# Splitting the FFN's tokens in place and turning them by DMA transposes, in a fused attention and FFN block

## What is computed

```python
x = x + attn(layernorm(x), W_qk, W_v, slope)      # scores = (x @ W_qk) @ x.T / sqrt(128)
x = x + ffn(layernorm(x), w_gate, w_up, w_down)   #   + (kpos - qpos) * slope, causal, softmax; v = x @ W_v.T
# ffn: h = silu(x @ wg.T) * (x @ wu.T); h @ wd.T   with wg, wu [384, 128], wd [128, 384] from int8-range integers / 127
```

## Time and profile before

| | us |
|---|---|
| median of 3 runs | 145.16 (144.49 to 145.37) |
| the profiled execution, its own time | 145.67 |
| its span, first to last instruction | 143.9 |
| PE busy | 122.8 (85% of the span) |
| DVE busy | 120.7 (84%) |
| ACT busy | 110.7 (77%) |
| POOL busy | 97.6 (68%) |

### The profile page before, as it was taken

The page is one execution under the profiler, slowest core; times in us unless marked ns, Lnnn a source line. Parts: engine busy times, 40 slices in busy tenths (PEclk is TensorE's granted clock), DMA queues, the critical chain, the costliest instruction groups (busy, mean ns, idle before and its releaser), DMA issues.

```text
span 143.9 us, 3450 instructions
## 1 busy us (share of the span) xinstructions
PE 122.8 (85%) x1215; PEld 91.9 (64%) x1215; DVE 120.7 (84%) x341; ACT 110.7 (77%) x251; POOL 97.6 (68%) x157
## 2 busy tenths in 40 slices
PE   0239658999999999999999998979998899999942
PEld 0028345867987769978779776657755656675541
DVE  0729989998697996969996969999879999988781
ACT  4034588999976999949999769985699978999830
POOL 6490769964993454992438943798999999646810
PEclk9999999999999999999999999999999999999995
DMA  4997000000000000000000000000000222022204
GB/s 129 221 244 190 0 0 2 7 2 0 5 0 0 5 0 2 5 0 0 0 5 0 5 0 2 2 5 0 5 0 0 77 77 66 12 73 77 77 0 146
DMA packets 9811, 5.18 MB, mean 36 GB/s; under 512 B 448, under 2 KB 9792, under 8 KB 9792
## 3 DMA queue, kind: packets, MB, share of 16 engines
q1 hardware_dynamic: 9792, 4.92, 12.2%
HBM read 2.82 MB, written 2.10 MB: 34 GB/s over the span
## 4 chain that ended last, share of the span: by engine, by line
PE 50%; DVE 23%; ACT 9%; POOL 7%; DMA 4%; issue 3%; SPq 2%; DVEq 0%
PE work_ps L556 7%; POOL hidden_lo L411 6%; PE attn_ps L571 5%; PE attn_ps L573 4%; PE attn_ps L572 4%; PE score_ps L504 4%; PE score_ps L506 4%; DVE probsT_lo L824 4%; PE score_ps L505 4%; DMA wd_int<-in_L_ffn_w_down_dram 4%; DVE biased L841 3%; PE score_ps L595 2%; PE score_ps L592 2%; DVE stats L726 2%; ACT silu L1069 2%
## 5 line engine op out<-in xcount | busy, mean ns | idle before, releaser
L571 PE MATMUL attn_ps<-v_hi,probsT_hi 128*128 128x128 f16 x144 | 25.8, 219 | 3.0 <-DVE xs L851 2.4
L824 DVE TENSOR_TENSOR probsT_lo<-work_ps,probsT_hi 128x512 f16<-128x512 f32 (+3 forms) x48 | 25.2, 552 | 3.5 <-ACT probsT_hi L1007 3.4
L1007 ACT CAST probsT_hi<-work_ps 128x512 f16<-128x512 f32 (+3 forms) x48 | 21.4, 484 | 7.7 <-PE work_ps L556 7.4
L992 ACT ACTIVATE probs<-biased,neg_max 128x128 f32<-128x128 f32 (+7 forms) x32 | 25.0, 783 | 1.9 <-DVE neg_max L841 1.9
L841 DVE CUSTOM_DVE_ANT_0 biased<-score_ps,bias,neg_score_scale 128x128 f32<-128x128 f32 (+7 forms) x32 | 25.8, 806 | 0.6 <-PE score_ps L506 0.6
L573 PE MATMUL attn_ps<-v_hi,probsT_lo 128*128 128x128 f16 x144 | 25.8, 219 | 0.0
L572 PE MATMUL attn_ps<-v_lo,probsT_hi 128*128 128x128 f16 x144 | 25.8, 219 | 0.0
L556 PE MATMUL work_ps<-ident,probs 128*128 128x128 f32 x144 | 21.4, 274 | 0.2 <-DVE probsT_lo L824 0.2
L411 POOL TENSOR_TENSOR hidden_lo<-hidden,hidden_hi 128x512 f16<-128x512 f32 x13 | 17.6, 1375 | 5.1 <-ACT hidden_hi L1075 5.1
L556 PEld LDWEIGHTS work_ps<-ident,probs 128*128 128x128 f32 x144 | 16.5, 141 | 3.2 <-DVE probsT_lo L824 0.5
L437 POOL TENSOR_TENSOR xT_lo<-whole,xT_hi 128x512 f16<-128x512 f32 x8 | 9.3, 1163 | 13.6 <-ACT whole L986 13.6
(11 more groups left out here) (135 smaller groups left out, 346.7 us busy)
## 6 DMA issues: line engine op xcount, KB each, us to landing
out_dram<-xs SPq DMA_DIRECT2D x7, 256.0 KB, 2.7
xs<-in_L_attn_x_dram SPq DMA_DIRECT2D x3, 512.0 KB, 7.4
xs<-in_L_attn_x_dram SPq DMA_DIRECT2D x2, 256.0 KB, 3.0
out_dram<-xs SPq DMA_DIRECT2D x2, 128.0 KB, 1.9
wgu_int<-in_L_ffn_w_gate_dram SPq DMA_DIRECT2D x1, 192.0 KB, 3.1
wgu_int<-in_L_ffn_w_up_dram SPq DMA_DIRECT2D x1, 192.0 KB, 3.4
wd_int<-in_L_ffn_w_down_dram SPq DMA_DIRECT2D x1, 192.0 KB, 5.1
wqk_in<-in_L_attn_W_qk_dram SPq DMA_DIRECT2D x1, 64.0 KB, 2.9
```

The lines of the kernel that those rows point to most:

```text
L571: pe.matmul(attn_ps[:, 0:D], p_hi, v_j, start=(j == 0), stop=False)
L824: dve.tensor_tensor(probsT_lo[:, i % 2, cols], work_ps[:, bank, 0:n], probsT_hi[:, i % 2, cols], ALU.subtract).then_inc(work_emptied, 1)
L992: act.activation(probs[:, i % 2, 0:n], biased[:, i % 2, 0:n], ACT.Exp, bias=neg_max[:, i:i + 1], scale=-1.0, accum_out=prob_sum[:, i:i + 1 ...
L1007: act.copy(probsT_hi[:, i % 2, CW * h:CW * h + n], work_ps[:, bank, 0:n]).then_inc(probsT_hi_ready, 1)
```

## The change

- `xn` gets two halves, by the parity of n. For LN2, ACT casts the normalised tokens where they lie, in SBUF, to `xn_hi` (`token_high`), POOL subtracts to `xn_lo` (`token_low`), and SP turns each of the two by a DMA transpose into `x2T_hi` and `x2T_lo`: 16 DMA transposes of 128x512 float16 (128 KB). They stand on SP's queue ahead of all stores of the result.
- PE's `transpose_x2`, ACT's `copy_x2_high` and DVE's `split_x2` go, and so do the fifth xT's transposes, copies and subtractions in the last round. The token casts of chunks 0 to 3 stand in steps 0 to 3 of the last round, those of chunks 4 to 7 behind the silus of chunks 0, 1, 3 and 4.
- LN2 of batch 0: its statistics move from round 2 (steps 0 to 3) to round 1 (steps 4 to 7), its work on POOL into round 2. LN2 of batch 1: statistics from the last round (steps 0 and 1) to round 2 (steps 1 to 4). LN2 of batch 2: from steps 4 and 5 of the last round, where they stood ahead of `add_attention`, to steps 0 to 3, behind it.
- POOL's order from the last round on: norm(5), the four token casts of chunks 0 to 3, norm(6), moments(7), the cast of chunk 4, centre(7), scale(7), hidden_low(1), the cast of chunk 5, hidden_low(2), hidden_low(3), the cast of chunk 6, hidden_low(4), the cast of chunk 7, and the rest. `pool_blocks(1)` falls from 2 to 1; DVE takes the other.
- `down` alternates between two PSUM banks, as the bank of the transposes is free.
- The order of the ring is one list (`ring`) with the same entries but the fifth xT, and the rest of the diff is the same code with plain integers.

```diff
+    ring = [(kind, 0, h) for kind, h in prologue] + [("P", 0, 0, 0)]
+    for b in range(B):
+        for i in range(TB):
+            nb, ni = (b, i + 1) if i + 1 < TB else (b + 1, 0)
+            if nb < B:
+                ring += [("P", nb, ni, h) for h in range(ni // CT + 1)]
+            ring += [(kind, b + 1, h) for kind, h in parts_at(b, i)]
...
+            for n in range(B, NROUND):
+                for h in range(HALVES):
+                    tiles = slice(CT * h, CT * (h + 1))
+                    for part, ready, o in ((xn_hi, xn_hi_ready, x2T_hi), (xn_lo, xn_lo_ready, x2T_lo)):
+                        sp.wait_ge(ready, split_before(n, h) + 1)
+                        sp.dma_start_transpose(o[:, HALVES * (n - B) + h, :].rearrange("p (t q) -> p t q", q=P),
+                                               part[:, n % 2, tiles, :].rearrange("p t d -> p (t d)"))\
+                          .then_inc(x2T_landed[n % 2][h], 16)
...
-                if isinstance(n, int) and n > B + 1:
-                    pool.wait_ge(x2T_filled, HALVES * (n - B - 1))
-                elif not (isinstance(n, int) and n == 0):
-                    pool.wait_ge(work_filled, place(n - 2, ("xT", HALVES - 1))[1] + 1)
+                if n >= B + 2:
+                    pool.wait_ge(xn_lo_ready, split_before(n - 1, 0))
+                elif n >= 2:
+                    pool.wait_ge(work_filled, filled(("xT", n - 2, HALVES - 1)))
...
+            def token_low(n, h):
+                tiles = slice(CT * h, CT * (h + 1))
+                pool.wait_ge(xn_hi_ready, split_before(n, h) + 1)
+                pool.tensor_tensor(xn_lo[:, n % 2, tiles, :], xn[:, n % 2, tiles, :], xn_hi[:, n % 2, tiles, :],
+                                   ALU.subtract).then_inc(xn_lo_ready, 1)
...
-            for b in range(B - 1):
-                nxt = (b + 1) % 2
-                for part in prologue:
-                    if by_pool(part):
-                        split_low(b + 1, nxt, *part)
-                norm(b + 2)
-            for part in prologue[:HALVES]:
-                split_low(B, B % 2, *part)
+            def split_lows(b, kind):
+                for h in range(HALVES):
+                    split_low(b, b % 2, kind, h)
+
+            for b in range(1, B - 1):
+                split_lows(b, "xT")
+                split_lows(b, "q")
+                norm(b + 1)
+            moments(B)
+            split_lows(B - 1, "xT")
+            centre(B)
+            split_lows(B - 1, "q")
+            scale(B)
             norm(B + 1)
-            moments(B + 2)
-            centre(B + 2)
+            for n in (B, B + 1):
+                for h in range(HALVES):
+                    token_low(n, h)
+            norm(B + 2)
             moments(B + 3)
-            scale(B + 2)
+            token_low(B + 2, 0)
+            centre(B + 3)
+            scale(B + 3)
             hidden_low(1, 1)
-            centre(B + 3)
+            token_low(B + 2, 1)
             hidden_low(2, 0)
-            scale(B + 3)
             hidden_low(3, 1)
-            for m in range(2, NCH // 2 - 1):
-                for par in range(2):
-                    hidden_low(2 * m + par, par)
-            for par in range(2):
-                hidden_low(NCH - 2 + par, par)
+            token_low(B + 3, 0)
+            hidden_low(4, 0)
+            token_low(B + 3, 1)
+            for c in range(5, NCH):
+                hidden_low(c, c % 2)
...
-                    if not (isinstance(c, int) and c < 2):
-                        pe.wait_ge(x2T_ready, c - 1)
+                    n, h = B + c // HALVES, c % HALVES
+                    pe.wait_ge(x2T_landed[n % 2][h], landed(n))
...
-            def transpose_x2(c, par):
-                pe.wait_ge(xn_ready, HALVES * B + c)
-                if not (isinstance(c, int) and c == 2):
-                    pe.wait_ge(x2T_ready, c - 2)
-                for j in range(CT):
-                    m = pe.transpose(x2T_ps[:, P * j:P * (j + 1)], xn[:, CT * par + j, :], ident[:, :])
-                m.then_inc(x2T_filled, 1)
-            def down(c, par, o=down_ps, tiles=range(CT)):
+            def down(c, par, o, tiles=range(CT)):
                 def product(with_lo):
-                    if not (isinstance(c, int) and c == 0):
+                    if c:
                         pe.wait_ge(pool_lo_ready, pool_blocks_to(c))
                     pe.wait_ge(vector_lo_ready, vector_blocks_to(c))
-                    if isinstance(c, int) and c == 0:
+                    if c == 0:
                         pe.wait_ge(attn_added, NT)
-                    elif not (isinstance(c, int) and c == NCH - 1):
-                        pe.wait_ge(result_ready, c)
+                    elif 1 < c < NCH - 1:
+                        pe.wait_ge(result_ready, c - 1)
...
                 for par in range(2):
                     gate_up(c + par, par, range(EARLY if first and par == 0 else 0, HB))
-                    if not final:
-                        transpose_x2(c + par + 2, par)
                     if not (first and par == 0):
-                        down(c + par - 1, 1 - par)
+                        down(c + par - 1, 1 - par, down_ps[1 - par])
...
+                if j == 0 and n not in (0, 1, B + 3):
                     dve.wait_ge(pool_step, steps_before(n) - N_STEPS + N_READ)
+                if j == 0 and B <= n < B + 3:
+                    dve.wait_ge(attn_added, TB * (n - B + 1))
...
+            def statistics_at(b, i):
+                first = {0: {2: 0}, 1: {3: 0, B: CT}, B - 2: {B + 1: 1}, B - 1: {B + 2: 0}}[b]
+                return [(n, i - k) for n, k in first.items() if k <= i < k + TB // 2]
...
-                    if final and i % (TB // 2) < HALVES:
-                        for j in range(CT):
-                            statistics(b + 2 + i // (TB // 2), CT * (i % (TB // 2)) + j)
...
                     add_attention(b, i)
-                    if not final and i < TB // 2:
-                        statistics(b + 2, 2 * i)
-                        statistics(b + 2, 2 * i + 1)
+                    for n, k in statistics_at(b, i):
+                        statistics(n, 2 * k)
+                        statistics(n, 2 * k + 1)
...
-            def split_x2(c, par):
-                dve.wait_ge(x2T_hi_ready, c - 1)
-                dve.tensor_tensor(x2T_lo[:, par, :], x2T_ps, x2T_hi[:, par, :], ALU.subtract).then_inc(x2T_ready, 1)
...
+            def token_high(n, h):
+                tiles = slice(CT * h, CT * (h + 1))
+                act.wait_ge(xn_ready, HALVES * n + h)
+                if n >= B + 2:
+                    act.wait_ge(x2T_landed[n % 2][h], landed(n - 2))
+                act.copy(xn_hi[:, n % 2, tiles, :], xn[:, n % 2, tiles, :]).then_inc(xn_hi_ready, 1)
...
+                    for part in parts_at(b, i):
                         copy_high(b + 1, nxt, *part)
+                    if final and i < 2 * HALVES:
+                        token_high(B + i // HALVES, i % HALVES)
...
-            def copy_x2_high(c, par):
-                act.wait_ge(x2T_filled, c - 1)
-                act.copy(x2T_hi[:, par, :], x2T_ps).then_inc(x2T_hi_ready, 1)
...
-                    if not final:
-                        copy_x2_high(c + par + 2, par)
+                    for n, h in {0: [(B + 2, 0)], 1: [(B + 2, 1)], 3: [(B + 3, 0)], 4: [(B + 3, 1)]}.get(c + par, []):
+                        token_high(n, h)
```

More of the change, by code:

```diff
@@ L12 @@
 AX_X = mybir.AxisListType.X
-ds = bass.ds
 P = 128
@@ L98, in preln_block, with parts_at @@
-    assert not any(by_pool(g) for g in middle[-NWORK:] + opening[-NWORK:])
-    VECTOR_TAKES, POOL_TAKES = (len(opening) * (1 - k) + (B - 1) * sum(by_pool(g) == k for g in middle)
-                                + sum(by_pool(g) == k for g in closing) for k in (False, True))
-    assert middle[-1] == opening[-1] == (0, 0)
+    NROUND = 2 * B
+    def parts_at(b, i):
+        return prologue[i - 1:i] if i and b < B - 1 else []
+    ring = [(kind, 0, h) for kind, h in prologue] + [("P", 0, 0, 0)]
@@ new lines, in preln_block, with bank_of, filled, by_pool @@
+    for b in range(B):
[4 more added lines that the diff above has]
+            ring += [(kind, b + 1, h) for kind, h in parts_at(b, i)]
+    ring_index = {key: n for n, key in enumerate(ring)}
+    def bank_of(key):
+        return ring_index[key] % NWORK
+    def filled(key):
+        return ring_index[key] + 1
+    def by_pool(key):
+        return key[0] in ("xT", "q") and key[1] > 0
@@ L352, in halves_of @@
             def halves_of(n):
-                return range(int(isinstance(n, int) and n == 0), HALVES)
+                return range(int(n == 0), HALVES)
             def moments(n):
@@ L538, in scores @@
                 if i in (0, 2):
[L540 to L541 removed]
+                    taken(("q", b, i // 2))
+                if t >= 2:
                     pe.wait_ge(biased_ready, t - 1)
```

163 lines of the change are left out of this document (61 added, 102 removed).

## The result

The changed kernel takes 147.78 us (median of 4 runs, 147.54 to 148.49), the kernel before 144.86 (144.49 to 145.37): 1.022 times the time, 95% interval 1.018 to 1.026. The forecast was 147.7, in a range of 145.4 to 149.6, and slower with a chance of 0.64. In a later comparison (17 runs of before, 6 of the changed kernel) it was 1.012 (1.006 to 1.017). The cause of the spread behind these figures is one of the findings. A ratio leaves out executions more than 1.5% above the fastest of the same kernel, in the later comparison the two longest of six, which is why 1.012 stands beside medians of 147.36 and 144.68 that make 1.019.

What follows compares the result with a forecast made beforehand. Prediction: PE bounds middle rounds, DVE the last, a cross-engine chain the FFN, with POOL's queue at its head. 145.16 + 1.0 (attention +0.1, FFN about 0.9) + 1.5 for the clock gives 147.7 us, range 145.4 to 149.6.

Steps and rivals of the forecast that it cites:

- Second round: Attention round 2: DVE's added statistics wait for POOL's moments(3) and delay PE; 1.1 us lost, bounds 0.4 to 1.6.
- Third round: Attention round 3: as many statistics as before, one step later, under cover of waits; 0 us.
- Last round: Last attention round: 8 statistics leave DVE, so step 4's addition comes sooner; -1.0 us, bounds -0.4 to -1.6.
- Head of the FFN: POOL's queue ahead of down(1): added cast, centre(7) and scale(7) make down(1) start at 115.7, 2.2 us later.
- Chunks and clock: FFN chunks at 4.1 or 4.35 us against 4.52 win back 1.2; PE's clock falling after the gap costs 1.5.
- rival B: PE's clock holds through the gap before down(1): 146.2 us; chance 0.24.
- Sum: Whole kernel: 145.16 + 1.0 without the clock, plus 1.5 for its fall, 147.7 us.
- A: The forecast itself: all terms including the clock's fall, 147.7 us; chance 0.45.
- C: DMA transposes of chunks 6 and 7 land late, over 4.1 us from the cast; at 6 us, 148.1 to 149.6; chance 0.18.
- the 0 of this term: DMA transposes in the FFN: landings up to 4.1 us cost nothing, 5.1 costs 1.0; taken as 0.
- D: Faster: round 2's wait is hidden and PE runs at its bare 3.95 per chunk; 144.0 us at full clock; chance 0.07.
- E: No change: gains of the last round and the chunks' pitch equal the losses, 145.2 us; chance 0.06.

Runs made afterwards that it cites:

- r1: Changed kernel, with LN2 of batch 0 given its own statistics buffer so DVE need not wait for POOL in the second round: 146.79 us, 1.008 of the kernel before.
- r5: Kernel before, with only the last round's layer-norm statistics moved behind add_attention instead of ahead of it: 147.11 us, 1.011 of the kernel before.
- r9: Changed kernel, with centre(7) and scale(7) on POOL put between the low parts of chunks 1, 2 and 3: 145.30 us, 1.004 of the kernel before.
- r12: Changed kernel with r9's POOL order, third statistics buffer, 18 idle tail transposes, one chunk-3 block moved POOL to DVE, later casts of chunks 6 and 7: 145.07 us.
- r0: The changed kernel run again with no edit: median 147.36 us over six executions.
- r2: Changed kernel, with 28 idle PE transposes ahead of down(1) into an unused bank: 146.09 us, 1.009 of the kernel before.
- r3: Changed kernel, with hidden_low(1) on POOL moved ahead of centre(7) and scale(7): 147.23 us, 1.016 of the kernel before.

## Why the prediction was right

**Second round.** Forecast 1.1, from 55.8 to 57.4 of standstill and four statistics; measured 1.05, a wait of 1.50, and r1 shows about 0.7 of it to be the wait. **Third round.** Forecast 0, measured 20.02 from 62.73 to 82.75, against the same before (timeline of PE before, from 62.12):

```profile
82.14 0.22 PE L571 MATMUL attn_ps<-v_hi,probsT_hi 128*128 128x128 f16 x1 [0.18 <-DVE xs L851]
```

**Last round.** Forecast -1.0 and a wait under 0.3; measured -1.04 and 0.32. What the prediction didn't see is that this gain alone, in the kernel before (r5), is idle time of PE a little later.

**Head of the FFN.** moments(7) was forecast at 104.95 and came at 104.15 + 0.44 = 104.59. The forecast had shifted the 104.80 of before, but there POOL came to it straight from centre(6), without a wait; in the changed kernel POOL was free and waited 2.30 for the statistics. The work behind it was forecast at 10.65 and took 11.1, scale(7) 0.9 too long and the two single blocks 0.2 too short each. The two errors, 0.36 too late and 0.44 too short, cancel, which is luck: down(1) was forecast at 115.7 and came at 115.30 + 0.44 = 115.74, its gap 3.31 for 3.3. The step that was mis-sized is the price of an operation on POOL while DVE does the same kind of work beside it. It is the step on which the later expectations (r9, r12) went wrong, too.

**Chunks and clock.** Without the clock, the gate_ups of chunks 3 to 7 were forecast at 117.1, 121.1, 125.8, 129.9 and 134.0. With the 0.44 they came at 118.27, 122.43, 127.20, 131.18 and 135.39: later by 1.2 to 1.4 each. That is the clock's fall, and 1.5 was said. The forecast's 1.5 was a choice between 0 and 3.95, and so near by luck in part: in r0's profiled execution the fall cost 1.4 more than in this one. r2, which takes only the fall away, ends at 146.09 where rival B stood at 146.2.

**Sum.** The forecast was 2.5 above the median of 145.16; measured are 2.9 (147.78 against 144.86) and 2.7 in the later comparison. The time of 147.7 is hit more closely than the difference, because the base was 0.3 lower. The 0.3 outside the span was in no term.

**Rivals.** A came. B is the changed kernel with a full clock, and r0 shows one execution in six of it at that clock, 145.34. C didn't come, by 0.1 and 0.4 us. The forecast took the store's 1.9 as the nearest row, and the two landings that counted took 4.1, the very bound up to which nothing was to be lost: the 0 of this term held by luck. D and E are excluded by the second round's wait. **Chances.** That the fall's length differs from one execution to the next was not in the forecast; the range held it (of r0's six executions, all but the one at 145.34).

## What to carry to other kernels

In a chain across engines, look at each in-order queue for what stands ahead of the operand that comes next: here 6.1 us of work needed later (1.16, 2.03 and 2.93) stood ahead of 1.15 us needed now, and less work on three engines made a slower kernel. To move that one piece ahead only moves the gap (r3); the long work has to be spread between the pieces that are needed (r9). A wait of TensorE such as the 3.31 us here costs more than itself, and not the same in each execution: measure such a kernel more often, and fill the gap with idle matmuls to price the clock by itself. A saving is only worth what arrives at the last engine: PE's 0.9 in r5 bought nothing.

## What the runs showed of the hardware

**The clock's fall isn't the same each time.** In the traces, gaps of TensorE of 3.31 (after, r0, r1) and 2.63 us (r5) in front of down(1) were followed by 0.50; one of 2.52 (r3, down(2)) and one of 2.60 (r9, the last down) were not. A gap of 1.94 or 1.95 us ahead of the last down was followed by a fall in before, after and r2, and not in r0 and r1. The changed kernel has its gap of 3.31 in every trace, yet one of r0's six executions had a mean clock of 1.000. At the end of after the clock was 1.00 for about another us behind the gap, then less; in r0 it stayed (stretches of after, then of r0):

```profile
141.00:142.00 1.00, 0.97 (x18) 1.00 (x19) 0.65 (x2) 0.00 (x0) 0.00 (x0) 1.00 0.00 0
142.00:143.00 1.00, 0.75 (x10) 0.48 (x7) 0.60 (x2) 0.00 (x0) 0.00 (x0) 0.58 0.43 140
...
143.00:144.00 1.00, 0.96 (x18) 0.79 (x15) 0.48 (x1) 0.00 (x0) 0.00 (x0) 1.00 0.05 17
```

**DVE and POOL slow each other.** A subtraction of 128x512 from SBUF by DVE takes 0.68 alone and can take 1.4 beside POOL (2.84 and 2.95 for two); POOL's pair of 128x512 (`centre`, `scale`) takes 2.04 alone and 2.49 or 2.93 beside DVE; operations of 128x8 take 0.20 and 0.73. Which of the two pays is not fixed. DVE's block and POOL's pair of chunk 6 ran beside each other in both of these (timelines of DVE and POOL, after, then r9):

```profile
135.82 0.69 DVE L928 TENSOR_TENSOR hidden_lo<-hidden,hidden_hi 128x512 f16<-128x512 f32 x1
134.80 2.72 POOL L408 TENSOR_TENSOR hidden_lo<-hidden,hidden_hi 128x512 f16<-128x512 f32 x2 [1.26 <-ACT hidden_hi L1058]
...
133.13 1.67 DVE L928 TENSOR_TENSOR hidden_lo<-hidden,hidden_hi 128x512 f16<-128x512 f32 x1
131.98 2.28 POOL L408 TENSOR_TENSOR hidden_lo<-hidden,hidden_hi 128x512 f16<-128x512 f32 x2 [1.12 <-ACT hidden_hi L1058]
```

In after POOL paid 0.4, in r9 DVE 1.0. The Trainium skill (SBUF — State Buffer, SBUF: two separate sides) says that the two share a pair of ports, which the one that starts first holds for its whole instruction while the other waits. The rows agree, and the prediction left it out.

**A DMA transpose** of 128x512 float16 from SBUF to SBUF lands 2.4 to 4.1 us after its issue (after; median 2.5 for the high parts, 3.6 for the low) and holds SP's queue for 1.2 to 1.4, two of the sixteen for 2.0 and 2.3. That is under the 5.2 of four in a row that the prediction weighed.
